# Hyperedge loop of a four-layer graph network: round sums copied out and added on GpSimd instead of kept in a PSUM bank

## The reference, cut to what matters

```python
h = x @ W
agg = jnp.einsum('ben,bnf->bef', alpha, h)                      # one row per hyperedge
beta = sigmoid((h @ a_gn)[:, None, :] + (agg @ a_ge)[:, :, None])
all_he = elu(beta[..., None] * h[:, None, :, :] + (1.0 - beta[..., None]) * agg[:, :, None, :])
se = tanh(elu(agg) @ fcW + fcb) @ av
coefs1 = softmax(where(H[None] > 0, se[:, None, :], NEG), axis=-1)
g = jnp.einsum('bne,benf->bnf', coefs1, all_he)                 # sum over a node's hyperedges
```

## Time and profile before

| | |
|---|---|
| median of 3 runs | 905.51 us (902.73 to 907.22) |
| profiled execution | 904.9 us, span 903.1 us |
| PE busy | 754.8 us (84%) |
| DVE busy | 479.8 us (53%) |
| ACT busy | 345.5 us (38%) |
| POOL busy | 289.3 us (32%) |
| the 8 rounds, about | 150 us to 240 us of the span |

### The profile page before, as it was taken

The page is one execution under the profiler, slowest core; times in us unless marked ns, Lnnn a source line. Parts: engine busy times, 40 slices in busy tenths (PEclk is TensorE's granted clock), DMA queues, the critical chain, the costliest instruction groups (busy, mean ns, idle before and its releaser), DMA issues. The chain is left out here.

```text
span 903.1 us, 10528 instructions
## 1 busy us (share of the span) xinstructions
PE 754.8 (84%) x3510; PEld 495.1 (55%) x3518; DVE 479.8 (53%) x1158; ACT 345.5 (38%) x724; POOL 289.3 (32%) x337
## 2 busy tenths in 40 slices
PE   3966977888898459899898993999999999939990
PEld 3646765666565358433232322787666666628880
DVE  1494254777357831245464666312778878820165
ACT  1741213545463121346353542222445564642110
POOL 0440001445446320001003149000556576730055
PEclk9967995999997579989998996899999999969995
DMA  8200011000000000000000001000000000000013
GB/s 277 70 24 1 1 32 62 2 1 0 1 1 1 0 1 1 1 0 1 1 0 1 0 5 45 1 1 1 1 1 0 1 1 1 1 0 1 1 24 70
DMA packets 12952, 14.39 MB, mean 16 GB/s; under 512 B 9680, under 2 KB 9680, under 8 KB 12896
## 3 DMA queue, kind: packets, MB, share of 16 engines
q1 hardware_dynamic: 11408, 11.61, 4.1%
q10 hardware_dynamic: 1488, 2.06, 0.7%
HBM read 11.57 MB, written 2.10 MB: 15 GB/s over the span
## 5 line engine op out<-in xcount | busy, mean ns | idle before, releaser
L1564 DVE SCALAR_TENSOR_TENSOR arena<-PS,WT,arena 128x128 f32<-128x128 f32 x320 | 111.2, 350 | 20.2 <-PE PS L1664 9.3
L1329 DVE TENSOR_REDUCE arena<-PS 128x1 f32<-128x1024 f32 x64 | 75.6, 1219 | 79.7 <-PE PS L1165 79.7
L1252 ACT ACTIVATE arena<-PS,arena 128x1024 f32<-128x1024 f32 x64 | 70.8, 1109 | 74.9 <-DVE arena L1329 74.9
L1503 ACT ACTIVATE SY<-PS,WT 128x128 f32<-128x128 f32 x192 | 56.5, 365 | 78.3 <-DVE arena L1564 78.3
L163 POOL TENSOR_TENSOR LN_Y<-LN_V,CN 128x16 f32<-128x16 f32 (+1 forms) x17 | 51.0, 2998 | 104.8 <-DVE LN_V L155 104.8
L1165 PE MATMUL PS<-arena 64*128 64x512 f32 x256 | 79.2, 636 | 4.6 <-ACT arena L1252 2.4
L1272 POOL TENSOR_TENSOR arena<-arena 128x128 f32<-128x128 f32 x32 | 12.9, 403 | 191.6 <-DVE arena L1333 191.6
L1183 PE MATMUL PS<-arena 128*64 128x512 f32 x256 | 64.2, 625 | 1.2 <-POOL arena L1272 1.1
L1654 PE MATMUL PS<-WH,KH 128*128 128x512 f32 x128 | 57.1, 446 | 1.4 <-DVE KL L1551 1.4
L1165 PEld LDWEIGHTS PS<-arena 64*128 64x128 f32 x256 | 28.9, 190 | 52.3 <-issue 33.4
L1655 PE MATMUL PS<-WL,KH 128*128 128x512 f32 x128 | 50.5, 395 | 0.0
(11 more groups left out here) (263 smaller groups left out, 1608.0 us busy)
## 6 DMA issues: line engine op xcount, KB each, us to landing
arena<-in_adj_tr SPq DMA_DIRECT2D x8, 512.0 KB, 8.3
arena<-in_x_tr SPq DMA_DIRECT2D x4, 512.0 KB, 9.3
arena<-in_x_nat SPq DMA_DIRECT2D x1, 2048.0 KB, 8.3
out<-arena SPq DMA_DIRECT2D x8, 256.0 KB, 3.0
arena<-in_w SPq DMA_DIRECT2D x2, 512.0 KB, 4.1
WT<-in_weights ACTq DMA_DIRECT2D x1, 739.0 KB, 8.6
arena<-in_h_tr ACTq DMA_DIRECT2D x2, 256.0 KB, 10.8
CN<-in_consts ACTq DMA_DIRECT2D x1, 507.0 KB, 5.2
```

The lines of the kernel that those rows point to most:

```text
L1252: act.activation(EF[2 * (i % RING) + par], banks("S", 2 * i + par).rearrange("p a c -> p (a c)"), ACT.Exp, bias=NMX[:, i, par:par + 1], ac ...
L1329: dve.tensor_reduce(NMX[:, i, par:par + 1], banks("S", 2 * i + par), AX.XY, ALU.max, negate=True).then_inc(max_ready, 1)
L1503: act.activation(groups(SY[:, n % SYS, :]), PS[:, pair_of_banks(t, j), d * F:(d + 1) * F], ACT.Copy, scale=WT[:, e:e + 1]).then_inc(sy_rea ...
L1564: dve.scalar_tensor_tensor(acc, PS[:, pair_of_banks(t, j), d * F:(d + 1) * F], WT[:, e:e + 1], acc, ALU.mult, ALU.add).then_inc(acc_step, 1)
```

## The change

The sums of a round no longer stay in PSUM. Each round's first scatter starts banks 4 and 7 afresh (`start=(c == A_)`) and the last closes them, so the two zero matmuls and their wait go, and so does the zero tile. At the end of each round, inside the loop, ACT copies bank 4 to `ROUND_SUM` (in `XX`, which a later block uses) and bank 7 to `ROUND_Z`, giving `acc_raw`; POOL then adds both into `ZS[:, t]` and `GN[:, t]`, giving `acc_out`. POOL clears `ZS` and `GN` once with two memsets ahead of the loops.

DVE makes the node matrix first in the round, ahead of the mixes, and no longer waits for PE's transposes of it, because `turn_nodes` now reads the copy `NSG`. `bend(A)` and `bend(C)` come later in DVE's round. On PE, `small_sums` stands ahead of `scatter(A)`, and `scatter(B)` behind the gather of A and `turn_nodes`.

What stays as it was: `high(t + 2)` and `low(t + 2)` are written behind tile t's loop, and PE waits for `hpl_ready` ahead of each tile's loop.

```diff
-        zero16 = sb("zero16", [P, 512], BF16)
...
-                pool.memset(zero16[:, :], 0.0).then_inc(zero_set, 1)
...
+        XX = sb("XX", [P, B, 2, F])
+        ROUND_SUM = XX[:, 0:B // 2, :, :].rearrange("p b k f -> p (b k f)")
+        ROUND_Z = sb("ROUND_Z", [P, B])
...
-                        ins = pe.transpose(PS[:, 6, tile(c)], NSF[:, c, :], ident)
+                        ins = pe.transpose(PS[:, 6, tile(c)], bits(NSG[:, c, :]), ident)
...
                 for t in range(NT):
-                    if t >= 1:
-                        pe.wait_ge(acc_out, t)
-                    pe.matmul(PS[:, 4, :], zero16[:, 0:P], zero16[:, :], start=True, stop=False, skip_group_check=True)
-                    pe.matmul(PS[:, 7, ZN_AT:ZN_AT + B], zero16[:, 0:P], zero16[:, 0:B], start=True, stop=False, skip_group_check=True)
                     pe.wait_ge(hpl_ready, min(t + 2, NT))
...
                             pe.wait_ge(w_ready, CHUNKS * j + (c + 1))
-                            return pe.matmul(PS[:, 4, :], NST[:, c, :], S1[:, c, :], start=False, stop=True, skip_group_check=True)
+                            if c == A_:
+                                pe.wait_ge(acc_raw, j + 1)
+                            return pe.matmul(PS[:, 4, :], NST[:, c, :], S1[:, c, :], start=(c == A_), stop=(c == C_), skip_group_check=True)
...
-                        scatter(A_)
                         pe.wait_ge(self_ready, j + 2)
                         small_sums(t_next)
+                        scatter(A_)
...
                         gather(t_next, B_)
-                        scatter(B_)
                         pe.wait_ge(z_ready, CHUNKS * j + 3)
                         gather(t_next, A_)
                         turn_nodes()
+                        scatter(B_)
                         scatter(C_)
...
+                        dve.wait_ge(nsg_ready, j + 1)
+                        from_first(at).then_inc(ns_half, 1)
+                        dve.wait_ge(ns_half, j + 2)
+                        to_last(at).then_inc(ns_ready, 1)
                         dve.wait_ge(be_ready, j + 1)
                         mix(B_, 1)
                         mix(A_, 2)
-                        dve.wait_ge(selg_ready, j + 1)
-                        dve.wait_ge(nt_ready, j + 1)
-                        from_first(at).then_inc(ns_half, 1)
                         shift(A_, 2)
-                        dve.wait_ge(ns_half, j + 2)
-                        to_last(at).then_inc(ns_ready, 1)
                         shift(B_, 1)
-                        bend(A_)
...
                         edges(k_next)
+                        bend(A_)
...
                     if t >= 1:
-                        dve.wait_ge(acc_out, t)
+                        dve.wait_ge(acc_out, first[t] + 1)
...
                         likely()
+                        act.wait_ge(acc_done, j + 2)
+                        act.wait_ge(acc_out, j + 1)
+                        act.activation(ROUND_SUM, PS[:, 4, :], ACT.Copy)
+                        act.activation(ROUND_Z[:, :], PS[:, 7, 0:B], ACT.Copy).then_inc(acc_raw, 1)
                     if t + 2 < NT:
                         high(t + 2)
-                    act.wait_ge(acc_done, first[t + 1] + 1)
-                    act.activation(GN[:, t, :], PS[:, 4, :], ACT.Copy)
-                    act.activation(ZS[:, t, :], PS[:, 7, ZN_AT:ZN_AT + B], ACT.Copy).then_inc(acc_out, 1)
...
                 low(1)
+                pool.memset(ZS[:, :, :], 0.0)
+                pool.memset(GN[:, :, :], 0.0).then_inc(acc_out, 1)
+                pool.wait_ge(acc_out, 1)
...
+                        pool.wait_ge(acc_raw, j + 2)
+                        pool.wait_ge(acc_out, j + 1)
+                        pool.tensor_tensor(ZS[:, t, :], ZS[:, t, :], ROUND_Z[:, :], ALU.add)
+                        pool.tensor_tensor(GN[:, t, :], GN[:, t, :], ROUND_SUM, ALU.add).then_inc(acc_out, 1)
                     if t + 2 < NT:
                         low(t + 2)
```

More of the change, by code:

```diff
@@ L457, in _ @@
                 link(dve.tensor_reduce(ae[:, :], AGM[:, :, :], AX.X, ALU.add))
-                dve.wait_ge(zero_set, 4)
+                dve.wait_ge(zero_set, 3)
                 for par in range(2):
@@ L615, in program @@
         iota = CN[:, C_IOTA:C_IOTA + ROUND].rearrange("p (c n) -> p c n", n=P)
-        SMALL_AT, ZN_AT = CHUNKS * E, 0
+        SMALL_AT = CHUNKS * E
         A_, B_, C_ = range(CHUNKS)
@@ L627, in program @@
                              "z_ready", "e_ready", "t_ready", "w_ready"))
-        acc_done, acc_out, rn_ready, g_done = (sem(s) for s in ("acc_done", "acc_out", "rn_ready", "g_done"))
+        acc_done, acc_raw, acc_out, rn_ready, g_done = (sem(s) for s in ("acc_done", "acc_raw", "acc_out", "rn_ready", "g_done"))
+        XX = sb("XX", [P, B, 2, F])
+        ROUND_SUM = XX[:, 0:B // 2, :, :].rearrange("p b k f -> p (b k f)")
+        ROUND_Z = sb("ROUND_Z", [P, B])
         def first_rounds(eng):
@@ L730, in _ @@
                         turn_nodes()
+                        scatter(B_)
                         scatter(C_)
                         for c in range(CHUNKS):
-                            ins = pe.matmul(PS[:, 7, ZN_AT:ZN_AT + B], NST[:, c, :], CC[:, c, :], start=False, stop=True,
+                            ins = pe.matmul(PS[:, 7, 0:B], NST[:, c, :], CC[:, c, :], start=(c == A_), stop=(c == C_),
                                             skip_group_check=True)
@@ L808, in _ @@
                         small_out()
-                        bend(C_)
                         dve.wait_ge(ts_ready, j + 2)
                         logits()
+                        bend(C_)
                     if t >= 1:
-                        dve.wait_ge(acc_out, t)
+                        dve.wait_ge(acc_out, first[t] + 1)
                         dve.reciprocal(ZS[:, t - 1, :], ZS[:, t - 1, :]).then_inc(rn_ready, 1)
-                dve.wait_ge(acc_out, NT)
+                dve.wait_ge(acc_out, first[NT] + 1)
                 dve.reciprocal(ZS[:, NT - 1, :], ZS[:, NT - 1, :]).then_inc(rn_ready, 1)
@@ L840, in likely @@
                     act.activation(XC[:, :, :], LG[:, :, :], ACT.Exp).then_inc(xc_ready, 1)
+                act.nop().then_inc(acc_raw, 1)
                 act.wait_ge(fold_ready, 1)
@@ L1358, in program @@
         X3 = node_major(3)
-        XX = sb("XX", [P, B, 2, F])
         ZH = rounded("ZH", 5 * SLOT, [P, NT, BF])
```

## The result

| | before | after |
|---|---|---|
| median of 4 runs | 904.12 us (902.12 to 907.22) | 957.63 us (955.06 to 958.6) |
| profiled execution, span | 903.1 us | 955.7 us |
| first to last copy of the sums, seven rounds | 75.8 us | 120.7 us |
| mean granted PE clock, whole span | 0.907 | 0.872 |

The ratio is 1.0575 (95% interval 1.0545 to 1.0604). The forecast was 932.0 us with a range of 921 to 942; the direction was right, and the time lies 15.6 us above the top of the range.

The account below looks back on a forecast made before the run. The prediction took PE as the bound, standing still at the top of each tile. Rounds +20.4, clock +7.5, head -2.4 and tail +1.6 gave +27.1 us on 904.9: 932 us, range 921 to 942.

Parts of the forecast that it names:

- The mechanism: At six tile changes PE waits for POOL's low, queued behind two adds that wait for ACT's copies; about 3.9 us.
- E to T: From the end of a round's last matmul (L733) to the next edge rows (L655): 4.2 us instead of 1.5.
- T to E at full clock: From a round's first edge rows to its last matmul's end: 10.1 us instead of 9.25.
- the idle spot: Between turn_edges and small sums, PE idle while ACT makes SELF: 0.7 us.
- The extra scatter in PE's way: Inside the round, scatter A comes on top of the time ACT makes SELF: 0.86 us a round.
- One fall costs 1.3 us: Price of one drop of PE's clock, from the old round starting at 197.23: 10.53 us instead of 9.25.
- The count of falls: One drop of PE's clock for each new 4.2 us pause, six in all.
- The rival with the longer low level: The chain holds but PE's lower clock lasts longer: +34.6 us, 939.5 us; chance 0.15.
- The head: Ahead of the first round: T 2.0 us earlier, scatter A 0.86 back, 1.25 gained without a clock fall; -2.4 us.
- Tail and rest: After the last round, adds follow the copies and POOL's last L914 ends later: +1.6 us before the barrier, nothing across it.
- seven rounds at full clock: Six rounds of 14.3 us and one of 10.4, 96.2 us against 75.8: +20.4 us.
- clock within them: One clock fall for each of six pauses, 6 x 1.25 us: +7.5 us, bounds 0 to 15 us.

Follow-up runs that it names:

- experiment 1: Changed kernel with sixteen unused 512-column matmuls where PE waits for hpl_ready at six tile changes; 932.5 us, 1.0295 against the kernel before.
- experiment 5: Kernel before with only PE's new order: small sums ahead of scatter A, scatter B behind the gather of A; 924.62 us, 1.0191.
- experiment 4: Kernel before with one wait added: POOL waits for the copy of the sums (acc_out) ahead of low(t + 2); 924.19 us, 1.0189.
- experiment 8: Changed kernel with the memsets of ZS and GN ahead of low(0) and low(1) instead of behind; 954.58 us, 1.054 against the kernel before.
- experiment 6: Changed kernel with two extra 512-column matmuls between turning the edges and small sums, nothing at the top; 944.43 us, 1.0456 against the kernel before.
- experiment 3: Changed kernel with high(t + 2) on ACT and low(t + 2) on POOL ahead of tile t's loop; 934.16 us, 1.0314 against the kernel before.

## Why the prediction missed

**Right.** The mechanism and its full-clock price. E to T is 4.06 us (4.2), T to E at full clock 10.09 (10.1, experiment 1), a round 14.2 (14.3), the idle spot 0.58 us (0.7). The wait stands at L656, put down to L895, six times. The extra scatter in PE's way is worth 0.80 us (0.86, experiment 5). In that the reading of the earlier trace rows held link by link.

**The step that failed is the price of one fall of the clock.** "One fall costs 1.3 us", six times, with 15 us as the upper bound. Measured against the 14.2 us of experiment 1 the six rounds cost 1.1, 5.0, 4.0, 5.1, 4.0 and 5.1 us: 24 us. The count of falls, one for each pause, was an estimate, since no row of before has a pause of 4 us inside the loop; the trace after shows it right, with the granted clock at 0.50 in a part of each of the six rounds. The price of 1.3 us was taken from one round of before, and finer windows of that round, which I should have read then, show how it differs: PE had no gap behind its pause, and had the level back at 1.00 in the window from 202, after some 3 us, when its small sums had just begun (L671 at 201.67).

```profile
199.00:200.00 1.00, 1.00 (x6) 0.74 (x5) 0.62 (x2) 0.00 (x0) 0.35 (x1) 0.50 0.03 8
...
201.00:202.00 1.00, 1.00 (x5) 0.48 (x3) 0.41 (x1) 1.00 (x3) 0.94 (x1) 0.56 0.00 0
202.00:203.00 1.00, 1.00 (x11) 1.00 (x10) 0.00 (x0) 0.17 (x1) 0.00 (x0) 1.00 0.00 0
```

In five of its six rounds the changed kernel came to the small sums, and to the idle spot ahead of them, with the level still low. I had priced that place as 0.86 us of work in a queue. The rival with the longer low level named this place ("a pause and then a half-idle stretch of PE") and still gave it only twice the old price, so even the range ended 15 us short. The idle spot alone doesn't account for the long falls: experiment 5 has falls behind 0.98 us of idle at the top and 0.58 us in the spot, but experiment 4 has long falls with no idle spot and PE busy throughout (9.00 of 9.00 us at 0.50).

**The head**: the first copy came 2.55 us later, not 2.4 earlier. T was early as forecast (150.92, predicted 151.3), but the clock did fall and stayed at 0.50 from 154 to about 164, where it had been down to 157.5 in before; the round took 15.43 us from T to E. The forecast had the fall gone with the pause. The memset had been taken as time on POOL only; it held DVE's L741 for 2.1 us beyond its 0.42, and the mixes came as much later (150.40 against 148.34). Without that hold this round ran at a mean clock of 1.00 in the one trace of experiment 8, so it may bear on the fall, though one execution doesn't prove it. That L741 ends 0.21 us behind the memset and behind the multiply is what the traces show; why DVE is held there, no view here shows.

**Tail and rest**: from E of the last round to the next block's first matmul 4.06 us (287.08 to L1033 at 291.14) against 1.97, +2.1 (predicted 1.6). The seventh round took 11.18 instead of 10.4, since PE waited 1.05 us for POOL's product at scatter A, which the prediction had ready in time: beside DVE's `bend` POOL's L921 took 1.49 us instead of 1.04 and its `CC` 0.68 instead of 0.23.

| term | predicted | measured |
|---|---|---|
| seven rounds at full clock | +20.4 | +20.6 |
| clock within them | +7.5 | +24.3 |
| head | -2.4 | +2.6 |
| tail | +1.6 | +2.1 |
| behind the barrier | 0 | +3.0 |
| sum (spans 903.1 and 955.7) | +27.1 | +52.6 |

The 3.0 us behind the barrier is what the spans leave over. 1.2 of it had come up by the next long pause of PE, some 85 us on; in that part PE comes out of the loop with a 4 us pause and runs at the low level, 0.50, from 290 to about 297, where before was at it for some 3 us (243 to 246). The rest came later, in code that is the same, and the stretch behind the loop differs by 10 us among the traces, so it need not be the change's. That the 24 us are the clock's is read from experiment 1, where the same six rounds took 22.7 us less with the chain as long as it was and a mean clock of 0.98 instead of 0.72. Why a fall lasted 3 us in one round and 10 or more in five is open: it goes with where the small sums fall in it, with the two wide matmuls of experiment 6 four of six rounds took 15.3 to 16.0 us, and in experiment 4 it lasted some 10 us twice with no idle spot.

## What to carry to other kernels

Before an accumulation is moved from PSUM to another engine, write down what is queued behind it on that engine and who waits for that: here it was not the sums but an unrelated `low` behind the adds on which PE stood. Price a pause of PE not by its length alone but also by the round that follows, at the lowest granted clock that the old trace shows (here 0.50, for ten of the fourteen microseconds from T to E), and keep that price as the bound: one cheap fall in the old trace (1.3 us) said little of the next (4.0 to 5.1 us). Look in that round for any further idle spot or run of narrow matmuls; an order that was dearer by 0.8 us of work had rounds that were dearer by 4.1 and 4.3 us more (15.5 and 15.7 against 11.4, experiment 5). Where a pause can't be removed, idle matmuls into a free bank are a quick test of how much of a loss is clock: sixteen of them took the mean clock from 0.72 to 0.98 and the total from 957.6 to 932.5 us here. And read what an edit did from the stretch that it touches: here the rest of the program moved by up to 10 us by itself.

## What the runs showed of the hardware

- A fall of the clock to 0.50 had two prices in the same loop: 1.1 us when the level was back by the small sums (0.50 from 171 to 174), 4.0 to 5.1 us when PE did them at 0.50, with 0.58 us of idle ahead of them (the changed kernel); with none ahead of them two rounds took 16.7 and 16.8 us against 11.9 (experiment 4). Of the 120.7 us of the seven rounds two wide matmuls in the spot gave back 7.7, sixteen in the pause 21.1, eight there 7.5.
- Falls followed short idle times in some rounds and not in others: 0.98 and 1.5 us at the top of a round in five of six (experiment 4), 0.98 us there and 0.58 inside in three (experiment 5). The runs of each spread by 10 to 15 us, the fastest at the highest granted clock (918.02 us at 0.904 and 932.76 at 0.891; 917.37 us at 0.901 and 927.62 at 0.888).
- DVE and POOL were slower side by side: `bend` on 128x512 took 1.35 us in the mean instead of 0.73, `low` 1.62 instead of 1.27, a 24-column multiply 0.68 instead of 0.23 (experiment 3). Beside a memset of 3.52 us on POOL a DVE `tensor_scalar` took 2.52 and 3.08 us instead of 0.42 and ended 0.21 us after it (changed kernel, experiment 8); beside POOL's multiply it took 1.1 us in the rounds of the changed kernel and also ended 0.21 us after it.
